# Expert tokens placed by one-hot matmuls and row gathers, and the up product untransposed and interleaved with the down product, in an attention-times-mixture-of-experts kernel

## The reference

```
xn = layernorm(x)
s  = attention(xn)            # 8 query heads of 128, one shared K and V head, causal, position table added to q and k
                              # then out @ Wo
f  = mixture of experts(xn):
       logits = xn @ router_w + router_b ; keep the 2 largest of 8 experts, softmax over these two
       h = relu(xn @ w1[e] + b1[e])     # 256 -> 1024
       y = h @ w2[e] + b2[e]            # 1024 -> 256
       sum of the two y by their gates
x  = x + s * silu(f)
```

## Time and profile before

| | |
|---|---|
| median of 3 runs | 1295.18 us (1293.9 to 1295.59) |
| profiled execution, its own time | 1303.78 us |
| its span | 1301.7 us |
| PE matmul busy | 1028.5 us, 79% |
| weight loads (PEld) busy | 720.7 us, 55% |
| DVE | 820.1 us, 63% |
| ACT | 508.0 us, 39% |
| POOL | 508.3 us, 39% |
| mean TensorE clock granted | 0.928 of full |

### The profile page before, as it was taken

How to read it: one execution, slowest core, us unless ns; L and a number is a source line. 1 busy time by engine, 2 the same in 40 slices (tenths; PEclk the granted TensorE clock), 3 DMA queues, 4 the chain that set the end, 5 groups by cost and what they waited for, 6 DMA issues and landing times.

```text
span 1301.7 us, 25468 instructions
## 1 busy us (share of the span) xinstructions
PE 1028.5 (79%) x9135; PEld 720.7 (55%) x9135; DVE 820.1 (63%) x1424; ACT 508.0 (39%) x1023; POOL 508.3 (39%) x558
## 2 busy tenths in 40 slices
PE   0542019988679889889999986998799999999995
PEld 0411005666546555556666653665566766777783
DVE  5671019996044444445555545899899988899962
ACT  1511017886111111111111213566566656566641
POOL 1437783000277767762000001345345443435444
PEclk9967559999889999999999998899999999999997
DMA  6052238889399999998788773999899997999992
GB/s 229 1 206 102 104 111 159 150 145 155 96 172 198 190 199 204 206 198 163 146 151 155 150 168 104 146 163 158 155 186 160 153 164 121 152 160 157 169 187 89
DMA packets 533305, 201.16 MB, mean 155 GB/s; under 512 B 495642, under 2 KB 520676, under 8 KB 532548
## 3 DMA queue, kind: packets, MB, share of 16 engines
q1 hardware_dynamic: 517904, 157.61, 67.3%
q0 software_dynamic: 12752, 38.68, 12.0%
q10 hardware_dynamic: 2532, 3.26, 0.7%
HBM read 48.35 MB, written 29.10 MB: 59 GB/s over the span
## 4 chain that ended last, share of the span: by engine, by line
PE 34%; DVE 20%; DMA 10%; issue 3%; ACT 3%; SPq 2%; POOL 0%; POOLq 0%; DVEq 0%; ACTq 0%
PE psY L1242 11%; PE psU L1230 10%; DMA hT<-hp 7%; DVE b_nmax L903 6%; DVE b_ph L944 6%; PE b_psO L736 3%; PE b_psS L717 3%; PE b_psJ L748 2%; DMA b_pT<-b_ph 2%; PE b_psS L759 2%; DVE b_outs L952 2%; PE b_psJ L673 2%; DVE b_psJ L915 2%; DVE b_Q L928 1%; SPq L1098 1%
## 5 line engine op out<-in xcount | busy, mean ns | idle before, releaser
L1030 POOL TENSOR_SCALAR b_ph<-b_pr,b_rrec 128x896 f16<-128x896 f32 (+4 forms) x120 | 111.9, 941 | 453.4 <-DVE b_rrec L934 417.3
L1242 PE MATMUL psY<-w_p,hT 128*128 x1704 | 208.3, 281 | 32.1 <-DMA hT<-hp 32.0
L1242 PEld LDWEIGHTS psY<-w_p,hT 128*128 128x128 f16 x1704 | 170.3, 101 | 75.2 <-issue 39.7
L1260 ACT ACTIVATE hp<-psU 128x1024 f16<-128x1024 f32 x71 | 72.7, 1024 | 351.9 <-DVE psU L1269 305.0
L1230 PE MATMUL psU<-w_p,bxT 128*128 x852 | 197.7, 382 | 14.7 <-DMA bxT<-expert_rows 11.1
L1269 DVE SCALAR_TENSOR_TENSOR psU<-psU,b1b 128x1024 f32<-128x1024 f32 x71 | 87.5, 1233 | 170.2 <-PE psU L1230 170.2
L736 PE MATMUL b_psO<-b_pT,b_vp 128*128 128x128 f16 x2592 | 165.0, 221 | 27.7 <-DMA b_pT<-b_ph 15.1
L808 ACT ACTIVATE b_pr<-b_psS,b_nmax 128x1024 f32<-128x1024 f32 (+1 forms) x192 | 140.4, 736 | 113.9 <-DVE b_nmax L903 113.4
L736 PEld LDWEIGHTS b_psO<-b_pT,b_vp 128*128 128x128 f16 x2592 | 150.5, 99 | 40.0 <-DVE b_outs L952 18.6
L717 PE MATMUL b_psS<-b_kp,b_Q 128*128 128x512 f16 (+3 forms) x864 | 166.4, 329 | 0.1
L944 DVE SCALAR_TENSOR_TENSOR b_ph<-b_pr,b_rrec,b_ph 128x1024 f16<-128x1024 f32 (+1 forms) x192 | 154.7, 836 | 0.0
(11 more groups left out here) (192 smaller groups left out, 1440.7 us busy)
## 6 DMA issues: line engine op xcount, KB each, us to landing
wstage<-in_L_ffn_w POOLq DMA_DIRECT2D x64, 256.0 KB
expert_outputs<-y SPq DMA_DIRECT2D x71, 128.0 KB, 2.6
x_sb<-in_L_attn_x SPq DMA_DIRECT2D x4, 1024.0 KB, 15.5
b1b<-in_L_ffn_b POOLq DMA_DIRECT2D x8, 512.0 KB
xn_transposed<-xT SPq DMA_DIRECT2D x1, 3072.0 KB, 9.3
b_pT<-b_ph SPq DMA_TRANSPOSE x192
b_x_row<-in_L_attn_x SPq DMA_DIRECT2D x24, 128.0 KB
out<-b_x_row SPq DMA_DIRECT2D x24, 128.0 KB, 1.9
```

What stands on the lines that cost most here:

```text
L1030: a = eng.tensor_scalar(ph[k % 4][:, 2 * o:2 * o + w], pr[k % 3][:, o:o + w], rrec[:, at:at + 1], 1.0, ALU.mult, ALU.mult)
L1242: mm = eng.matmul(psY[n % 2][:, 0:D], hT[n % 3][:, a * HT + g, :], weight(n, 2 * W1 + (2 * g + b) * D, D), start=(k == 0), stop=(k == 3 * ...
```

## The change

- Stretch 1: no `free`. From each pair's slot its block `q_f` and its row in the block `r_f` are also kept as numbers, and `xp` is stored in HBM in token order (`xp_d`, 4 MB in four DMAs of SP).
- Attention of batch 0: no `send`, no zero rows. POOL makes for each of the 64 groups of 128 pairs two one-hot matrices (row in block, 128x128; block times token number, 128x71), three groups a step, in steps 0 to 21; PE multiplies them in head 6 (`place`, 64 matmuls of 71 columns into `psJ`), which gives `who`: for each slot its token. DVE copies it out in step 35. The 8 pieces of expert 0 are split during steps 22 to 36, loaded by SP now. The high half of steps 1, 3 and 4 goes from ACT to POOL, as in the other batches. At the end POOL gathers the rows of the first 8 blocks from `xp_d` to SBUF (`gather`), and SP writes them to `expert_rows` (`keep`).
- Experts: POOL does `gather(n)` and one `split` in turn for n = 8 to 63, then gathers alone; SP does `keep(n)` and one `stage` in turn. ACT issues the transposed loads of `bxT` and the stores of y. The up product has a 128x128 piece of `w_p` stationary and the 128 tokens moving: 48 matmuls of 128 columns, and its result needs no transpose. Its matmuls are interleaved with those of the down product of block n-2, six to three, in 8 groups. ACT adds the bias (now one number a partition) with the relu in 8 instructions of 128x128 (fp32, to SBUF), DVE makes the halves from it. `b1b` and `hT` with its DMA transposes are gone.

```diff
+    def gather(eng, n):
+        if n >= 4:
+            eng.wait_ge(st_[n % 4], 16 * (n // 4))
+        eng.indirect_dma_start(rowx[n % 4][:, :], None, xp_d, bass.IndirectOffsetOnAxis(ap=who[:, n:n + 1], axis=0)).then_inc(gx_[n % 4], 16)
+    def keep(eng, n):
+        eng.wait_ge(gx_[n % 4], 16 * (n // 4 + 1))
+        eng.dma_start(rows_d[n * BLK:(n + 1) * BLK, :], rowx[n % 4][:, :]).then_inc(st_[n % 4], 16)
...
-    BY_ACT = (0, 1, 2, 3, 4) if first else (0, 2)
+    BY_ACT = (0, 2)
...
+            def place(a):
+                if a == 0:
+                    eng.wait_ge(jl_, len(jobs.order))
+                if a % PER == 0:
+                    eng.wait_ge(oh_, a // PER + 1)
+                mm = eng.matmul(psJ[:, 0:NBLK], oh_r[:, a, :], oh_q[:, a, :], start=(a == 0), stop=(a == COLS - 1))
...
-            def send(r):
-                s, c = r % 2, r // 2
-                eng.indirect_dma_start(rows_d, bass.IndirectOffsetOnAxis(ap=pos[:, s, c:c + 1], axis=0),
-                                       v["xp"][:, c, :, :].rearrange("p h d -> p (h d)"), None).then_inc(v["r_s"], 16)
+            def one_hot(a):
+                i, c = a // NT, a % NT
+                eng.tensor_scalar(oh_r[:, a, :], v["lanes"], v["r_f"][:, i, c:c + 1], None, ALU.is_equal)
+                mm = eng.tensor_scalar(oh_q[:, a, :], v["units"], v["q_f"][:, i, c:c + 1], v["ids"][:, c:c + 1],
+                                       ALU.is_equal, ALU.mult)
...
-            for n in range(NBLK):
-                up(n)
-                if n >= LAG:
-                    down(n - LAG)
+            def up(n, g, k):
+                a, b = PASSES[k // DC]
+                c = k % DC
+                mm = eng.matmul(psU[n % Z][:, g // 4, (g % 4) * P:(g % 4 + 1) * P], weight(n, a * W1 + c * H + g * P, P),
+                                bxT[n % X][:, 2 * b + c, :], start=(k == 0), stop=(k == 3 * DC - 1))
+            def down(n, g, k):
+                a, b = PASSES[k]
+                mm = eng.matmul(psY[n % 2][:, 0:D], hp[n % Z][:, a, g, :], weight(n, 2 * W1 + (2 * g + b) * D, D),
+                                start=(g == 0 and k == 0), stop=(g == HT - 1 and k == 2))
+            for n in range(NBLK + LAG):
...
+                for g in range(HT):
+                    for k in range(3):
+                        if n < NBLK:
+                            up(n, g, 2 * k)
+                            up(n, g, 2 * k + 1)
+                        if m >= 0:
+                            down(m, g, k)
```

More of the change, by code:

```diff
@@ L615, in attention @@
             sr = [sb(f"s_row{i}", [P, D], F32) for i in range(3)]
+            assert area.at <= v["gap_at"][0][0]
+            xTb = [v["xTb_next"], Arena(nc, v["gap_at"][0][1]).take("xTb_other", [P, 2 * DC, T], F16)]
+            area = Arena(nc, v["gap_at"][1][1])
+        ph = [sb(f"ph{i}", [P, 2 * T], F16) for i in range(2)]
+        if not first:
+            area = Arena(nc, v["gap_at"][2][1])
             q_at = area.at
@@ L779, in _ @@
                         project(*jobs.order[q], psJ[:, :]).then_inc(jm_, 1)
+                    if first and n == HEADS - 2:
+                        for a in range(i * COLS // 5, (i + 1) * COLS // 5):
+                            place(a)
                     if i == 4 and not first and n > QT:
@@ L1061, in _ @@
                     high(k - 1)
-                if not first:
+                if first:
+                    for a in range(k * PER, min(COLS, (k + 1) * PER)):
+                        one_hot(a)
+                    if k >= SPLIT and (k - SPLIT) % 2 == 0 and (k - SPLIT) // 2 < PIECES:
+                        v["split"](eng, (k - SPLIT) // 2)
+                else:
                     if i == 1 and n >= 2:
@@ L1132, in _ @@
             if first:
+                for p in range((LAST - SPLIT) // 2, PIECES):
+                    v["stage"](eng, p + 2)
+                for n in range(v["AHEAD"]):
+                    v["keep"](eng, n)
                 for s in range(4):
@@ L1208, in _ @@
             eng.dma_start(v["wo_late"][:, :, :, :], v["wo_d"]).then_inc(v["xl0"], 16)
-            for n in range(NBLK - LAG - 1, NBLK):
-                store(n)
         @block.tensor
@@ new lines, in store @@
+            def store(n):
+                eng.wait_ge(yb_, n + 1)
+                eng.dma_start(y_v[:, n, :], y[n % 3][:, :]).then_inc(y_o[n % 3], 16)
+            for n in range(X):
+                load(n)
+            for n in range(NBLK):
+                e = expert(eng, n)
+                for half in range(2):
+                    eng.wait_ge(up_, 2 * n + half + 1)
+                    if n >= 2:
+                        eng.wait_ge(hl_, 2 * (n - 2) + half + 1)
+                    for g in range(4 * half, 4 * half + 4):
+                        a = eng.activation(h32[n % 2][:, g, :], psU[n % Z][:, half, (g % 4) * P:(g % 4 + 1) * P], ACT.Relu,
+                                           bias=bias[:, ds(e * HT + g, 1)], scale=1.0 / WS)
+                    a.then_inc(rl_, 1)
+                if n + X < NBLK:
+                    load(n + X)
+                if n > LAG:
+                    store(n - LAG - 1)
@@ L1262, in _ @@
+            for n in range(NBLK - LAG - 1, NBLK):
+                store(n)
         @block.vector
```

248 lines of the change are left out of this document (111 added, 137 removed).

## The result

The changed kernel takes 1352.02 us (median of four runs, 1347.65 to 1355.53) against 1294.88 us of the kernel before on the same chip (1293.9 to 1295.59): a ratio of 1.044, 95% interval 1.0405 to 1.0475. The forecast was 1314 us. Its direction held, and its size was 38 us short. The profiled execution took 1355.53 us, with a span of 1353.7.

What follows compares the result with a forecast made beforehand. Batch 0 was held up by the scatter burst, the experts bound by PE, then by its address queue. Span 1301.7 - 83 + 5 + 95 + 2 = 1321, then + 2.1 - 8.6 = 1314 us; range 1282 to 1378.

Steps and rivals of the forecast that it cites:

- POOL's new work in batch 0: Attention of batch 0: one-hots, high halves and splits on POOL would add 5 us (0 to 15).
- rival D: Batch 0: POOL's high halves late all through heads 0 to 4, +15 us in place of +5; no separate chance given.
- the nearest row: Batch 0: one-hots priced like POOL's 128x128 high half in the profile, mean 525 ns, giving 3.2 us a step.
- the forecast's own range: Whole kernel: blocks of 7.0 to 7.7 us (-17, +28) and batch 0 between -5 and +10 give 1284 to 1352 us; 73%.
- rival B: Experts: PE's clock falls for a third of each block, adding 62 us, 1376 us in all; chance 10%.
- Burst gone, -83.1 us: Batch 0: without the burst of scatters, head 0 takes batch 1's 22.1 us in place of 105.2.
- The experts, +95 us: Experts: 48 addresses at 0.125 us plus reading the expert make blocks of 7.3 us; 533 us in place of 437.7.
- Held-up completions in the experts, +2 us: Experts: single gathers between splits now and then delay PE's completions; +2 us taken, bounds nothing and 40 us.
- Rival A: Experts: address work hidden, PE's array sets the pace; block 5.5 us, 124 us less, 1190 us; chance 12%.
- Rival C: Batch 0: burst not the cause, or POOL's new order replaces it; the 83 us hole stays, 1397 us; chance 5%.
- From the profiled execution to the median: Whole kernel: the median of runs was taken to lie 8.6 us below the profiled execution's time.
- The rule that was weighed: Batch 0: by the skill's port rule the burst could not stop PE; removing it might give nothing, 1397 us.

Runs made afterwards that it cites:

- run 4: The changed kernel with all high halves of batch 0 made by ACT again: 1319.49 us, ratio 1.0219 to the kernel before.
- run 1: The kernel before, its 64 row scatters of batch 0 sent two a step instead of back to back: 1233.11 us, ratio 0.955.
- run 3: The kernel before, its 64 + 7 indirect row DMAs replaced by plain DMAs of the same bytes, tokens reaching wrong experts: 1228.54 us.
- run 5: The changed kernel with every block using expert 0's weights at a constant address, so output of one expert only: 1248.0 us.
- run 7: The kernel before, up product's weights moved in pieces of 128 columns instead of 512, 48 addresses a block: 1402.72 us.
- run 8: The kernel before, up product in pieces of 256 columns instead of 512, 32 addresses a block: 1311.9 us.
- run 10: Run 4's kernel with high-half down products merged into matmuls of 512 columns, 8 addresses there instead of 16: 1254.19 us, 0.9696 of the kernel before.
- run 2: The kernel before, scatters two a step and the seven zero-row scatters spaced one a step too: 1228.26 us, ratio 0.9487.
- run 6: The kernel before with every block using expert 0's weights at a constant address, output of one expert only: 1279.37 us.

## Why the prediction was wrong in size

The step that failed is "POOL's new work in batch 0: +5 us (0 to 15)". Batch 0 lost 31.9 us in heads 1 to 6, 4.5 in head 7 and the rows, and 1.3 in head 0: 37.7 us, 33 more than forecast, of the 38 that are missing. Its mechanism was seen, as rival D ("POOL high halves late all through heads 0 to 4"), and priced at +15.

Two things were wrong in the sum. The high halves that come to POOL were not added: 3.2 us of one-hots in a step of 3.3 us leaves nothing for them, so the step was over its limit by the prediction's own numbers. With 0.7 us of high halves a step that is 0.6 us over, some 13 us in 21 steps, still inside its 0 to 15. The larger part is the price: a one-hot pair takes 1.448 us, not 2 x 0.525 by the nearest row, 1.2 us more a step and 25 in 21 steps.

Together POOL has 5.0 us of work in each step of 3.3: 1.7 x 21 = 36 us as an upper estimate. Heads 0 to 4, which hold these steps, were 27.5 us longer than in run 4; POOL starts 12 us ahead of head 0's maxima, which the estimate leaves out. The other 5.7 us came in heads 5 and 6, 4.2 of them in head 5, where a high half stands behind a split that waits for its load and DVE's low halves take longer; the prediction had neither. Run 4 shows that all of this needs the high halves on POOL: with them on ACT, the 33 us of heads 0 to 6 are gone. Of the 4.5 us in head 7 and the rows it gives back 2.4 (50.5 us against 52.9); the other 2.1 have no shown cause.

**The range** held, but not by its sum. The measured 1352 us is at the upper end of the forecast's own range, 1284 to 1352, and the stated range went on to 1378 for rival B, a falling clock, which did not come. That is luck. The lower end was also summed wrongly: a block of 7.0 us gives 69 x 0.3 = 21 us less and not 17, and with batch 0 at -5 that is 1288 us.

**Burst gone, -83.1 us:** right, -81.8 for head 0. The cause was right too (runs 1 and 3).

**The experts, +95 us:** right, +99.8. 48 addresses a block, 3408 in all, 7.3 us a block. Run 5 takes the addresses away and the pace with them, runs 7 and 8 add addresses to the kernel before and the pace follows, and run 10 gives their price. The array's own pace, 0.22 us for three matmuls in run 5, makes 24 x 0.22 = 5.3 us, near the 5.5 of the prediction.

| kernel | addresses a block | starts of up products, first to last, us | a block | a block, 620 to 700 us |
|---|---|---|---|---|
| before | 24 | 412.4 | 5.8 | 5.2 |
| run 8, before with pieces of 256 | 32 | 426.2 | 6.0 | 5.5 |
| run 10, after with a wide down product | 40 | 452.3 | 6.4 | 6.3 |
| run 7, before with pieces of 128 | 48 | 511.0 | 7.2 | 7.3 |
| after | 48 | 519.4 | 7.3 | 7.3 |
| run 5, after, constant | 0 | 413.7 | 5.8 | 5.8 |

The means of the kernel before and of run 8 hold a first half in which the DMAs set the pace. The last column is free of it: 80 us, by PE's matmuls that start in them (551, 702, 813, 793, 787 and 988), times the matmuls of a block (36, 48, 64, 72, 72, 72). All six have a clock of 1.00 there.

**Held-up completions in the experts, +2 us:** small, as forecast. Where POOL gathers in a row, from 520 to 570 us, 309 up products start in place of 327, 2.8 us. **Rival A** is out: it needed 5.5 us a block. **Rival B** is out: the clock is 0.98 and 1.00 in the experts. **Rival C** is out: no hole is left. The prediction's 0.1 us for two more waits in the queue was not measured by any run. **From the profiled execution to the median**, 8.6 us were taken over from the kernel before, and it was 3.5: 5 us of the miss have no cause in the kernel.

**The rule that was weighed** says that among the engines' ports only the pair shared by VectorE and GpSimd causes contention, and that PE never waits (the Trainium skill, SBUF — State Buffer, "SBUF: two separate sides"). The rows were the better guide: the hole went with the burst. They don't contradict that section either: what DVE waited for until 174.64 us is the completion of a product that PE had started at 114.96 us and that lasts 2.74 us. Nor is it explained by the path that the DMAs take: the Trainium skill puts plain and indirect DMAs of GpSimd on the same one (DMA: Bandwidth & Descriptors, "SWDGE vs HWDGE vs iDMA"). In run 3 the plain ones brought no wait for "remote" in batch 0. What holds them up stays open.

## What to carry to other kernels

An operand of PE whose place is known only at run time has a price on PE's own queue, by distinct address and not by column. Count the addresses in a block before cutting a product into narrower pieces; put halves that are used together side by side, so that one address serves both.

Before giving an engine new work in a step, add up all that it then does in that step, the work that comes with it too, against the step's length; a sum that is over by a little is paid again in every step.

If an engine seems to wait for a product that ended long ago, look at what POOL issues at that moment. Indirect DMAs back to back held up PE's completions for tens of microseconds; spaced over the steps they left no such wait above 1.4 us, and the heads were 13 us longer than undisturbed (run 2).

## What the runs showed of the hardware

- Each address that depends on a register, with one matmul that uses it, costs 0.114 to 0.136 us on PE's queue (run 10 against run 4: over all blocks, and in the steady stretch of 620 to 670 us with 384 and 327 up products). Reading the register took a median of 0.99 us in the kernel before and 0.30 in the changed one. How far the queue runs ahead doesn't settle it alone: with constant addresses it was 1.00 in run 6 and 0.30 in run 5.
- 71 indirect DMAs of 128 rows in a row lengthened head 0 by some 82 us through PE's late completions. The same bytes in plain DMAs brought no such wait, though POOL issued them every 0.53 us in place of 1.28. Of run 1's 71, 64 were spaced, and the two waits of over 10 us that were left went when the other seven were spaced too (run 2).
- The size of a small POOL instruction says little of its time: a one-hot of 128x71 (compare and multiply) takes as long as one of 128x128 (compare alone), medians of 621 and 600 ns, while high halves of 128x128 took a mean of 366 ns in the same kernel. So the nearest row by size was no price for a one-hot. The means of the one-hots, 784 and 664 ns, and the longest, 1752 and 1592 ns, lie well above their medians. The Trainium skill says that a GpSimd instruction and certain VectorE instructions (in a two-port mode, or with two inputs in SBUF) lock a shared port pair for a whole instruction (SBUF — State Buffer, "SBUF: two separate sides"). The spread agrees, but no run here tells it from another cause.
